# Attention of a transformer block in two-head steps, scores and P times V in float32 on halves of the array

## What is computed

```
x = x + 0.5 * ffn(layernorm(x))         # gelu(x @ w1 + b1) @ w2 + b2
x = x + attn(layernorm(x))
x = x + 0.5 * ffn(layernorm(x))         # the same weights again
# attn: q, k, v = split(x @ w_qkv), 16 heads of 64
sim = (q * 64**-0.5) @ k.T + rel * slope[head]      # rel = -|i - j|
attn = softmax(where(causal, -max, sim))
out  = (attn @ v) @ w_out + b_out
```

## Time and profile before

| | us |
|---|---|
| median of 3 runs | 2592.37 (2589.94 to 2592.82) |
| profiled execution, its own time | 2591.63 |
| span of its trace | 2589.8 |
| PE busy | 2481.1 (96%) |
| DVE busy | 2029.6 (78%) |
| ACT busy | 1622.8 (63%) |
| POOL busy | 705.9 (27%) |

### The profile page before, as it was taken

The page is one execution under the profiler, slowest core; times in us unless marked ns, Lnnn a source line. Parts: engine busy times, 40 slices in busy tenths (PEclk is TensorE's granted clock), DMA queues, the critical chain, the costliest instruction groups (busy, mean ns, idle before and its releaser), DMA issues.

```text
span 2589.8 us, 46603 instructions
## 1 busy us (share of the span) xinstructions
PE 2481.1 (96%) x16256; PEld 2248.2 (87%) x16256; DVE 2029.6 (78%) x5222; ACT 1622.8 (63%) x3672; POOL 705.9 (27%) x1130
## 2 busy tenths in 40 slices
PE   6999999999999999999999999999999999999997
PEld 5888889888898888888888888888888889888896
DVE  6877969779697786968869687796877969779684
ACT  4856838467384764837658385583856838467383
POOL 1322313223232222313224132231322313223231
PEclk9999999999999999999999999999999999999998
DMA  4615326063360623506244161441715326063260
GB/s 136 153 25 125 88 49 151 14 139 74 70 143 1 153 60 90 123 18 146 50 105 108 25 157 32 115 98 30 159 25 127 86 53 150 11 139 74 68 136 9
DMA packets 103817, 227.71 MB, mean 88 GB/s; under 512 B 18080, under 2 KB 36768, under 8 KB 103584
## 3 DMA queue, kind: packets, MB, share of 16 engines
q1 hardware_dynamic: 103584, 224.73, 38.1%
HBM read 14.95 MB, written 8.39 MB: 9 GB/s over the span
## 4 chain that ended last, share of the span: by engine, by line
PE 79%; DVE 12%; DMA 3%; ACT 3%; issue 2%; POOL 1%; SPq 0%; DVEq 0%; ACTq 0%
PE psA L324 23%; PE psC L324 20%; PE psD L324 16%; PE psB L324 10%; PE psB L456 9%; DMA stack<-qk 3%; DVE gl L713 3%; DVE ptl L713 2%; DVE P L794 1%; DVE xn L743 1%; DVE xtl L713 1%; PE psB L349 1%; DVE gh L772 1%; ACT gt L597 1%; DVE ol L713 1%
## 5 line engine op out<-in xcount | busy, mean ns | idle before, releaser
L974 POOL TENSOR_SCALAR P<-P,rs 128x512 f32<-128x512 f32 (+3 forms) x1024 | 534.0, 534 | 1195.8 <-DVE rs L784 1195.8
L611 ACT ACTIVATE P<-P,mx 128x512 f32<-128x512 f32 (+3 forms) x1024 | 570.0, 558 | 252.1 <-DVE mx L794 252.1
L794 DVE CUSTOM_DVE_ANT_0 P<-psA,dist 128x512 f32<-128x512 f32 (+3 forms) x1024 | 440.3, 486 | 42.1 <-PE psA L324 40.3
L713 DVE TENSOR_TENSOR ptl<-psB,pth 128x512 fp32r<-128x512 f32 (+1 forms) x512 | 410.3, 816 | 30.0 <-ACT pth L652 27.7
L324 PE MATMUL psA<-stack 128*128 128x512 f32 (+3 forms) x2048 | 380.7, 328 | 28.3 <-DMA stack<-qk 28.2
L324 PEld LDWEIGHTS psA<-stack 128*128 128x128 f32 x2048 | 321.4, 190 | 57.5 <-DMA stack<-qk 34.4
L456 PE MATMUL psB<-ident,P 128*128 128x128 f32 x2560 | 328.9, 276 | 23.2 <-POOL P L974 22.3
L652 ACT ACTIVATE pth<-psB 128x512 fp32r<-128x512 f32 (+1 forms) x512 | 342.5, 702 | 4.5 <-PE psB L456 1.4
L456 PEld LDWEIGHTS psB<-ident,P 128*128 128x128 f32 x2560 | 285.0, 141 | 54.6 <-POOL P L974 33.5
L597 ACT ACTIVATE gt<-psA,b1c 128x512 f32<-128x512 f32 x256 | 174.4, 688 | 186.1 <-PE psA L324 184.2
L713 DVE TENSOR_TENSOR gl<-gt,gh 128x512 fp32r<-128x512 f32 x256 | 208.5, 814 | 8.8
(11 more groups left out here) (120 smaller groups left out, 6280.1 us busy)
## 6 DMA issues: line engine op xcount, KB each, us to landing
stack<-qk SPq DMA_DIRECT2D x512, 256.0 KB, 3.6
stack<-qk SPq DMA_DIRECT2D x512, 128.0 KB, 3.5
x<-in_L_attn_x SPq DMA_DIRECT2D x16, 512.0 KB, 4.3
out_y<-x SPq DMA_DIRECT2D x16, 512.0 KB, 3.9
raw<-in_L_ffn_w SPq DMA_DIRECT2D x2, 512.0 KB, 5.6
raw<-in_L_ffn_w SPq DMA_DIRECT2D x1, 1024.0 KB, 9.0
rawq<-in_L_attn_w_qkv SPq DMA_DIRECT2D x1, 1024.0 KB, 7.7
rawk<-in_L_attn_w_qkv SPq DMA_DIRECT2D x1, 1024.0 KB, 9.8
```

Source lines behind the costliest of these rows:

```text
L611: e.activation(p, p, ACT.Exp, bias=mx[:, r, i:i + 1], scale=-1.0, accum_out=sm[:, r, i:i + 1]).then_inc(s_ex.sem, 1)
L713: return e.tensor_tensor(dst, src, hi.bitcast(F32), ALU.subtract)
L794: e.tensor_tensor_reduce(out=P[h % 2][:, cs], in0=psA[:, cs], in1=dist[:, T - w:T], scale=-SLOPE[h], scalar=BIG, op0=ALU.add, op1=ALU.min, ...
L974: e.tensor_scalar(p, p, rs[:, s % 4, i:i + 1], 1.0, ALU.mult, ALU.mult).then_inc(s_nz.sem, 1)
```

## The change

All work of attention goes in steps of two heads (a pair, `c`, 8 for each sequence). Q, K, V, P and its transpose `PT` are held in plain float32, without parts. A scores product has 64 rows of contraction: head 0 of the pair uses rows 0 to 63 of the array, head 1 rows 64 to 127, one MATMUL a block and head, and they write to different banks of `psS`. In P times V the weights are 64 columns wide: head 0 writes partitions 0 to 63, head 1 partitions 64 to 127 of one bank. The stacking DMAs, the low parts of q, k, v and P, and the addition of halves are gone; ACT copies the projections and the result once, DVE copies the transposes (five a pair, of 512 columns each). PSUM is parted into `psS`, four banks for the scores, and `psR`, a ring of four banks that everything else takes in the order in which PE writes (`bank_for` waits for the reader of the use four places before). The projections, feed-forward products and the output projection keep their three fp32r products. The layer norm's `xn` has four places. Hidden tile 5 moves ahead of the last values, so two tiles follow attention and not three.

```diff
-    qk = place("qk", [128, 4, T], F32R, R)
-    stack = [place(f"stack{i}", [128, 3, T], F32R, R + 8192 + 6144 * i) for i in range(2)]
-    v = [place(f"v{i}", [128, NT, 4, 128], F32R, R + 20480 + 8192 * i) for i in range(2)]
-    P = [place(f"P{i}", [128, PW], F32, R + 36864 + 4 * PW * i) for i in range(2)]
-    pth = [place(f"pth{i}", [128, PW], F32R, R + 47104 + 8 * PW * i) for i in range(2)]
-    ptl = [place(f"ptl{i}", [128, PW], F32R, R + 47104 + 4 * PW + 8 * PW * i) for i in range(2)]
...
+    qk = [place(f"qk{i}", [128, 2, T], F32, QK + 4096 * i) for i in range(2)]
+    v = [place(f"v{i}", [128, NT, 4, DH], F32, V + 4096 * i) for i in range(2)]
+    P = [place(f"P{i}", [128, 2, PW], F32, PP + 8 * PW * i) for i in range(2)]
+    PT = [place(f"PT{i}", [128, 2, PW], F32, PT_AT + 8 * PW * i) for i in range(2)]
...
+    def score_block(h, i):
+
+        bank = (h, 0) if i in (3, 1) else (2 + h, 384 if i == 0 else 0)
+        at_col = 512 * bank[0] + bank[1]
+        return psS[:, at_col:at_col + 128 * (i + 1)]
+
+    ring = []
+
+    def bank_of(use):
+        n = ring.index(use) % 4
+        return psR[:, 512 * n:512 * n + 512]
...
+    EARLY = 6
...
+    def turn_shape(part):
+
+        if part == "both j2":
+            return slice(0, 2), KBASE[2], 256
+        h = 0 if part.startswith("even") else 1
+        return slice(h, h + 1), 512 if part.endswith("j13") else 0, 512
...
-            def stack_head(b, h):
-
-                c, i = h // 2, h % 2
-                src = qk[64 * i:64 * i + 64, :, :].bitcast(F32)
-                dst = stack[i]
...
-                for half in range(2):
-                    e.dma_start(dst[64 * half:64 * half + 64, 1:3, :].bitcast(F32), src[:, 1:3, :]).then_inc(s_sk[i].sem, 16)
-                e.wait_ge(s_pl.sem, s_pl.at((b, ("q", c))))
-                e.dma_start(dst[0:64, 0, :].bitcast(F32), src[:, 0, :]).then_inc(s_sq[i].sem, 16)
-                e.dma_start(dst[64:128, 0, :].bitcast(F32), src[:, 3, :]).then_inc(s_sq[i].sem, 16)
...
+            def bank_for(use):
+
+                ring.append(use)
+                if len(ring) > 4:
+                    kind, *key = ring[-5]
+                    if kind == "proj":
+                        e.wait_ge(s_pc.sem, s_pc.at(tuple(key)))
...
+            def scores(b, c, blocks):
+                n = pairs.index((b, c))
+                e.wait_ge(s_pc.sem, s_pc.at((b, ("q", c))))
+                for i in blocks:
                     w = 128 * (i + 1)
-                    dst = psA[:, QBASE[i]:QBASE[i] + w]
-                    qs = sk[:, 0, i * 128:i * 128 + 128]
-                    mm(dst, qs, sk[:, 1, 0:w], True, False)
-                    mm(dst, qs, sk[:, 2, 0:w], False, True).then_inc(s_qk.sem, 1)
+                    for h in range(2):
+                        if i == 1:
+                            e.wait_ge(s_tt.sem, s_tt.at((b, c, 3, h)))
+                        elif n > 0:
+                            e.wait_ge(s_tt.sem, s_tt.at((*pairs[n - 1], 1 if i == 3 else 0, h)))
+                        hs = slice(64 * h, 64 * h + 64)
+                        mm(score_block(h, i), qk[c % 2][hs, 0, i * 128:i * 128 + 128], qk[c % 2][hs, 1, 0:w],
+                           True, True).then_inc(s_qk.sem, 1)
...
+            def turn(b, c, part):
+                dst = bank_for(("turn", b, c, part))
+                if part == "both j2":
+                    e.wait_ge(s_nz.sem, s_nz.at((b, c, 1, 2)))
+                    where = [(h, 2, i, 256 * h + 128 * (i - 2)) for h in range(2) for i in (2, 3)]
...
+            def values(b, c):
+                pv = bank_for(("values", b, c))
+                e.wait_ge(s_pc.sem, s_pc.at((b, ("v", c // 2, 1))))
+                e.wait_ge(s_tc.sem, s_tc.at((b, c, TURNS[-1])))
...
-                    mm(pv[:, 128 * j:T], lhs, pth[h % 2][:, ks], j == 0, False)
-                    last = mm(pv[:, 128 * j:T], lhs, ptl[h % 2][:, ks], False, j == NT - 1)
+                    for i in range(2):
+                        last = mm(pv[64 * i:64 * i + 64, 128 * j:T], v[(c // 2) % 2][:, j, 2 * (c % 2) + i, :],
+                                  PT[c % 2][:, i, ks], j == 0, j == NT - 1)
...
+                    if more and c == NC:
+                        up(1, b + 1, [2])
...
+                    if more and c == NC + 1:
+                        up(1, b + 1, [4, 5])
...
+                    if more and c == NC - 1:
+                        up(1, b + 1, [0, 1])
...
-            def half(b, h):
-                e.wait_ge(s_pv.sem, s_pv.at((b, h)))
-                src = bk(bank_of(("values", h)))[64:128, :]
-                dst = o[64 * (h % 2):64 * (h % 2) + 64, h // 2, :]
-                e.activation(dst, src, ACT.Copy).then_inc(s_oc.sem, 1)
...
+            def out_copy(b, c):
+                e.wait_ge(s_pv.sem, s_pv.at((b, c)))
+                e.activation(o[:, c, :], bank_of(("values", b, c)), ACT.Copy).then_inc(s_oa.sem, 1)
...
+            def turned(b, c, part):
+                e.wait_ge(s_tp.sem, s_tp.at((b, c, part)))
+                if c >= 2:
+                    e.wait_ge(s_pv.sem, s_pv.at((b, c - 2)))
+                heads, col, w = turn_shape(part)
+                src = bank_of(("turn", b, c, part)).rearrange("p (h n) -> p h n", n=w)
+                e.tensor_copy(PT[c % 2][:, heads, col:col + w], src).then_inc(s_tc.sem, 1)
...
-            def turned_lo(b, h, part):
-                ps = PARTS[part]
-                e.wait_ge(s_hp.sem, s_hp.at((b, h, part)))
-                residue(ptl[h % 2][:, ps], psB[:, ps], pth[h % 2][:, ps]).then_inc(s_lo.sem, 1)
...
+                        if more and c == NC - 1:
+                            ln_lo(1, b + 1, 0)
+                        biased(b, c, 0)
+                        if c == 0 and b == 0:
+                            split_weight_lo("wout")
+                        if c == 0 and b > 0:
+                            add3(b - 1, 3)
+                        biased(b, c, 1)
+                        inverse(b, c, 1)
+                        if more and c == NC - 1:
+                            ln_lo(1, b + 1, 1)
+                    if more and c == NC:
+                        gelu_split(1, b + 1, [0, 1])
+                    if 1 <= c <= NC:
+                        for part in TURNS[:4]:
+                            turned(b, c - 1, part)
+                    if c < NC:
+                        inverse(b, c, 0)
+                    if 1 <= c <= NC:
+                        turned(b, c - 1, TURNS[4])
```

More of the change, by code:

```diff
@@ L181, in build @@
     s_tt = Signal("tt_done", per_block)
-    s_rc = Signal("rc_done", [(b, h, half) for b, h in heads for half in (1, 0)])
-    s_lo = Signal("lo_done", per_part)
-    s_oa = Signal("oa_done", heads)
-    s_pl = Signal("pl_done", proj)
+    s_rc = Signal("rc_done", [(b, c, half) for b, c in pairs for half in (1, 0)])
+    s_tc = Signal("turned_copied", per_turn)
     s_ll = Signal("ll_done", units)
@@ L362, in up @@
                 for m in ms:
-                    if m >= 3:
-                        e.wait_ge(s_gl.sem, s_gl.at((f, b, m - 3)))
+                    dst = bank_for(("up", f, b, m))
+                    if m == 0:
+                        e.wait_ge(s_ll.sem, s_ll.at((1 if f == 1 else 3, b, 1)))
                     cs = slice(m * 128, m * 128 + 128)
-                    last = three(bk(m % 3), [(w1h[:, k, cs], w1l[:, k, cs], xth[:, k, :], xtl[:, k, :])
-                                             for k in range(NK)])
+                    last = three(dst, [(w1h[:, k, cs], w1l[:, k, cs], xth[:, k, :], xtl[:, k, :])
+                                       for k in range(NK)])
@@ new lines, in turn @@
+            def turn(b, c, part):
[3 more added lines that the diff above has]
+                    where = [(h, 2, i, 256 * h + 128 * (i - 2)) for h in range(2) for i in (2, 3)]
+                else:
+                    h = 0 if part.startswith("even") else 1
+                    e.wait_ge(s_nz.sem, s_nz.at((b, c, h, 1)))
+                    if part.endswith("j0"):
+                        where = [(h, 0, i, 128 * i) for i in range(NT)]
+                    else:
+                        where = [(h, 1, i, 128 * (i - 1)) for i in range(1, NT)] + [(h, 3, 3, 384)]
+                for h, j, i, col in where:
+                    src = P[c % 2][:, h, QBASE[i] + 128 * j:QBASE[i] + 128 * j + 128]
+                    last = e.transpose(dst[:, col:col + 128], src, ident[:, :])
+                last.then_inc(s_tp.sem, 1)
@@ new lines, in attention @@
+                for c in range(NC + 3):
+                    if c >= 3:
+                        out_copy(b, c - 3)
+                    if c < NC:
+                        if more and c == NC - 1:
+                            ln_hi(1, b + 1, 0)
+                        exps(b, c, 3)
+                        if c + 1 < NC:
+                            proj_copy(b, ("k", c + 1))
+                        if more and c == NC - 1:
+                            ln_hi(1, b + 1, 1)
```

(16 more changed lines are left out.)

542 lines of the change are left out of this document (172 added, 370 removed).

## The result

The changed kernel took 2595.99 us (median of 20 runs, 2594.89 to 2601.18), the kernel before 2591.81 in the runs beside it (2589.94 to 2595.12): a ratio of 1.0016, interval 1.0009 to 1.0023. That is no difference by the bound of the prediction (0.2%), where 2694 was forecast. The profiled execution's span is 2594.8 us, against 2589.8.

A forecast was written before the change was run, and what follows sets the result against it. PE was taken to bound the kernel. Part products, edges and form changes +95 us, seams -28, +14 and +21, made +102 on 2591.6, or 2694 us, with its own range 2590 to 2830 and a chance of 52%.

The forecast's parts named there:

- What bounds the kernel: Middle of attention: PE alone bounds the kernel before, 11.56 us for a pair of heads with no wait in it.
- The part products: Scores and values of a pair: four float32 passes on halves working side by side, 4.27 us, where 5.08 was before.
- Edges of the groups: Scores and values: only one half of the array works at group edges, 1.05 us a pair, bounds 0 and 1.15.
- half a block's time between the starts: Sign of the forecast in scores and values: two heads' products of a block start that far apart, not a whole.
- Changes of form: PE switching between full array and halves: five changes a pair at 0.1 us each, 0.5 us, within 0 to 1.35.
- rival (1): Scores and values: PE's queue mostly hides edges and form changes, 4.6 us a pair, 2538 or 2500 us total; chance 20%.
- the two cases: Scores and values above or below 5.03 us a pair: the forecast of 2694 us, or rival (1) with its lower times.
- The seams: Between sequences: stacking DMA waits gone, -28 us; last pair's step, +14; one hidden tile less before output projection, +21.
- DVE, ACT and POOL: In a pair: 7.0, 6.6 and 4.17 us busy, far under PE's 12.3, so they cost nothing.
- rival (4): The ring of banks: copies come late, PE waits about 0.5 us in each step, 2760 us in total; chance 10%.

The follow-up runs named there:

- experiment 4: Changed kernel with queries and keys held as fp32r, so that their low parts are left out: 2428.8 us, ratio 0.937.
- (3): Changed kernel with both heads on the same half of the array, once in scores (2863.1 us) and once in values (2877.9 us).
- experiments 1: Changed kernel with all products of head 0 of a group ahead of all of head 1, in scores and values: 2910.1 us, ratio 1.123.
- 2: Changed kernel with two products of head 0 ahead of two of head 1, in scores and values: 2606.1 us, ratio 1.0053.
- experiment 5: Changed kernel with score blocks and transposes reordered for two more changes of the array's form in each of 112 pairs: 2631.1 us, ratio 1.015.
- experiment 7: Changed kernel with three hidden tiles behind attention instead of two: 2558.7 us, ratio 0.9869.
- experiment 9: The three-tile kernel of experiment 8, with DVE's reciprocal of half 1 behind the first four copies of transposes in the last pair's step: 2578.4 us, ratio 0.9951.
- experiment 8: Changed kernel with the layer norm's second high and low parts earlier in the last pair's step: 2600.6 us; also with three hidden tiles behind attention: 2563.0 us.
- experiments 6: Changed kernel with the fourth score block behind the values, for two fewer changes of form in a pair: 2625.4 us, ratio 1.0126.

## Why the prediction was wrong

- **What bounds the kernel**: right. PE carries 88% of the chain, and 0.04 us on a pair instead of 0.74 is nearly the whole error: 0.70 x 128 = 90 of the 98 us between 2694 and 2596. The other 8 less are a balance: 18 us more by the clock, which no term had, against some 26 less. Of these, 6 are PE's waits (+0.6 measured, +7 forecast), and about 20 lie outside the middle pairs, at the start, in the last sequence and in the pairs next to a seam, and were not taken apart.
- **The part products**: right. Four passes (experiment 4), both halves side by side (3), 4.27 us of columns for a pair. A clean group of scores takes 1.93 for 1.71 of columns, and values 2.30 for 2.13.
- **Edges of the groups**: here it failed. From "the second head's product of a block can't start before all of the first head's has been issued" I took that half of the first block is spent alone, 1.05 us a pair. The sentence says nothing of how far the issue runs ahead. A product for a free half begins while up to three earlier MATMULs have not begun (experiments 1 and 2), and with the heads in turn both first products begin within 0.01 us of each other (1039.30), where half a block's time between the starts had been named as the sign. The term is about 0. Experiment 1 shows that it can be 2.39 in another order, so the thought was sound, but not for the order that the diff has.
- **Changes of form**: mis-sized, in the other direction. 0.1 each was forecast, from the row of a first product that is 0.09 late. The last product ahead of the change pays about as much, so 0.16 to 0.18 (experiment 5). For five changes that is 0.8 to 0.9 and not 0.5, within the bounds of 0 to 1.35 that stood there. Most of it lies inside the pieces that I have called clean: (0.22 + 0.20 + 0.17) around 4.27, and 0.19 on the k tile. Scores and values take 4.86, not 5.32; with the 0.19 and 0.06 on the transposes the pair is 0.03 above the before's, 0.04 by the starts.
- **The rivals**: rival (1) put its turning point at 5.03 us for scores and values "with all their edges". Its mechanism held for the edges, and that had 20%. Its size didn't, since the forms cost 0.84 in all: 4.86 and 0.25 outside make 5.11, just past that point, and the time came out between the two cases. Edges and forms together stood at 1.55 and measure 0.84. I had given no case to edges that vanish beside forms at their full price, and the result lay in my range only by its lower end. By its own working (+7 on 2592, with a pair at 0) that end would be 2599 and not 2590, and the result lies under it.
- **The seams**: right in kind, and nearly in size. Gone are 28.2 and 22.3 us. The wait for `xtl` is 30.3 (forecast 36), that for `ol` grew by 19.8 (forecast 21). The sum of all waits changed by +0.6 where +7 was forecast; the first and the last sequence account for the difference (4.5 and 2.6 us less).
- **The clock**: missing, +18.1 us (the kernel before has one such drop, 1.7). I priced the new wait of 2 us by its length alone. Without it the changed kernel would stand at about 2578, some 0.5% under the one before: an estimate, from 2596 less 18.1.
- **DVE, ACT and POOL**: right, and no wait of the ring's copies stands in the middle pairs (0.3 us for `PT` in the whole run), so rival (4) is out.

## What to carry over

Where two halves of the array work at once, put their products in turn in the list, or at most two float32 products and two. Price a change of the array's form on both of its sides. Price a wait of PE of about 2 us by what the granted clock does behind it as well, which can cost almost as much again, and ask of each wait removed which queue the moved instruction now blocks, and beside which instruction of POOL a DVE instruction comes to lie.

## What the runs showed that I had not expected

- A MATMUL for a half that is free begins while three earlier ones, held by the other half, have not begun; a fourth holds it (2606 with two products and two, 2910 with three or four in a row).
- The Trainium skill says in "TensorEngine Tiling (Array Packing)", Key Properties, that a change of mode drains TensorE. The runs agree in that each change costs, and put it at 0.16 to 0.18 us between halves and the full array.
- The granted clock fell to 0.50 for 3.4 us, beginning 0.4 to 1.7 us after PE had taken up work again behind a wait of 2.0 us, and cost up to 1.7 us, in 12 of 15 sequences of the changed kernel. The length of the wait at that place does not decide it: 2.4 us in experiment 5 (8 of 15), 2.0 in experiment 7 (2 of 15), 1.7 in experiment 9 (8 of 15, every second one), 1.5 in the two runs of experiment 8 (13 and 4 of 15). The regular orders suggest that it matters where in time the wait falls. That is a guess; no experiment changed it alone, and what decides is open.
- Two kinds of DVE instruction took about 2.1 us longer where they began beside a long addition on POOL (1024 columns a partition): `gl` 2.75 and not 0.69 (experiment 9, 15 of 15), `gh` 2.52 and not 0.42 (experiments 6 and 8, 15 of 15 each). The layer norm's low part `xtl`, which reads from PSUM, kept its 0.69 in the 18 places beside it. That the addition is the cause is read from these coincidences; no experiment took it away.
